# A transformer layer on eight cores: the attention output projection moved into the attention loop

## The reference

```python
x = x + attn(layernorm(x))        # x: (8, 2048, 2048), 16 heads of 128, 4 K/V heads
x = x + ffn(layernorm(x))
# attn: q, k = rotate(x @ w.T + b); v = x @ wv.T + bv
#   scores = q @ k.T * 128**-0.5 + tril(ones)    (added, so all 2048 keys count)
#   out = softmax(scores) @ v;  return out @ wo.T + bo
# ffn: gelu(x @ proj1.T + b1) @ proj2.T + b2     (hidden size 8192)
```

## Time and profile before

| | |
|---|---|
| median of 3 runs | 3598.46 us (3597.36 to 3599.26) |
| the profiled execution, its own time | 3603.3 us |
| its span, slowest of 8 cores | 3601.8 us (the others from 3589.8) |
| granted TensorE clock, mean by core | 0.964 to 0.967 |
| busy over the span | PE 3154.4 us (88%), DVE 1423.4 (40%), ACT 1010.7 (28%), POOL 37.6 (1%) |
| moved by DMA | 385.32 MB, 107 GB/s on average |

### The profile page before, as it was taken

How to read it: one execution, slowest core, us unless ns; L and a number is a source line. 1 busy time by engine, 2 the same in 40 slices (tenths; PEclk the granted TensorE clock), 3 DMA queues, 4 the chain that set the end, 5 groups by cost and what they waited for, 6 DMA issues and landing times.

```text
span 3601.8 us, 51951 instructions; the slowest of 8 cores (3589.8 to 3601.8 us)
## 1 busy us (share of the span) xinstructions
PE 3154.4 (88%) x19893; PEld 1623.8 (45%) x20240; DVE 1423.4 (40%) x2425; ACT 1010.7 (28%) x1836; POOL 37.6 (1%) x64
## 2 busy tenths in 40 slices
PE   4599978888888888994999999999819999999999
PEld 1244445556556555441444444444404444444444
DVE  2512247777777775224122231322241222312223
ACT  3334456666666663113100101001021001010010
POOL 1000000000000000000000000000000000000000
PEclk8799999999999999997999999999959999999999
DMA  5232200000000001761656656566726565565666
GB/s 198 85 82 76 76 24 2 2 2 2 2 2 2 2 2 50 203 171 47 158 155 149 151 150 152 151 152 168 210 88 156 150 152 150 152 152 152 151 162 190
DMA packets 622179, 385.32 MB, mean 107 GB/s; under 512 B 7153, under 2 KB 605553, under 8 KB 617842
## 3 DMA queue, kind: packets, MB, share of 16 engines
q1 hardware_dynamic: 613874, 348.42, 38.2%
q0 software_dynamic: 8064, 33.56, 2.6%
HBM read 356.79 MB, written 25.17 MB: 106 GB/s over the span
## 4 chain that ended last, share of the span: by engine, by line
PE 73%; ACT 10%; DVE 7%; issue 5%; DMA 3%; DVEq 0%; ACTq 0%; SPq 0%; POOLq 0%
PE psh L960 25%; PE pso L980 24%; PE psqk L411 8%; ACT xn L566 7%; PE pso L670 6%; PE pvps L529 6%; DVE xn L586 3%; PE ps_t L515 2%; DMA xstg<-xT 2%; PE psvt L362 1%; DMA xn<-r1T 1%; PE sc L505 1%; ACT qbuf L545 1%; DVE t L837 1%; DVE qbuf L840 1%
## 5 line engine op out<-in xcount | busy, mean ns | idle before, releaser
L960 PE MATMUL psh<-qbuf,p1bf 128*128 128x512 bf16 x4014 | 884.9, 380 | 80.9 <-DVE p1bf L903 76.4
L980 PE MATMUL pso<-qbuf,p2bf 128*128 128x512 bf16 x4014 | 880.8, 379 | 16.2 <-ACT qbuf L996 11.9
L960 PEld LDWEIGHTS psh<-qbuf,p1bf 128*128 128x128 bf16 x4096 | 401.6, 98 | 563.2 <-issue 82.8
L566 ACT ACTIVATE xn<-sc 128x896 bf16<-128x896 f32 (+7 forms) x736 | 553.5, 773 | 308.6 <-PE sc L505 255.4
L980 PEld LDWEIGHTS pso<-qbuf,p2bf 128*128 128x128 bf16 x4096 | 400.2, 98 | 496.8 <-issue 15.4
L996 ACT ACTIVATE qbuf<-psh,b1f 128x1024 bf16<-128x1024 f32 x128 | 142.6, 1114 | 1400.1 <-PE psh L960 1400.1
L903 DVE CAST p1bf<-p1stg 128x2048 bf16<-128x2048 f32 x128 | 156.9, 1227 | 691.6 <-PE psh L960 616.3
L937 DVE CAST p2bf<-p2stg 128x2048 bf16<-128x2048 f32 x128 | 157.1, 1227 | 620.6 <-PE pso L980 529.7
L505 PE MATMUL sc<-kbuf,qbuf 128*128 128x512 bf16 x897 | 265.5, 380 | 97.3 <-ACT xn L566 75.2
L586 DVE COPY xn<-ps_t 128x2048 bf16<-128x2048 bf16 x256 | 312.2, 1220 | 95.7 <-PE ps_t L515 95.7
L515 PE MATMUL ps_t<-ident_s,xn 128*128 128x128 bf16 x4096 | 270.8, 219 | 82.7 <-DVE xn L586 78.3
(11 more groups left out here) (86 smaller groups left out, 1146.4 us busy)
## 6 DMA issues: line engine op xcount, KB each, us to landing
p1stg<-p1T SPq DMA_DIRECT2D x128, 1024.0 KB, 8.5
p2stg<-p2T SPq DMA_DIRECT2D x128, 1024.0 KB, 6.3
wstg<-wqT SPq DMA_DIRECT2D x16, 1024.0 KB, 6.3
wstg<-woT SPq DMA_DIRECT2D x16, 1024.0 KB, 11.4
xblk<-xT SPq DMA_DIRECT2D x16, 1024.0 KB, 7.1
xstg<-xT SPq DMA_DIRECT2D x8, 1024.0 KB, 6.9
xstg<-xT POOLq DMA_DIRECT2D x8, 1024.0 KB, 6.6
wstg<-wvT SPq DMA_DIRECT2D x8, 1024.0 KB, 5.5
```

Source lines behind the costliest of these rows:

```text
L566: last = s.activation(p_sb[u % 3]()[:, il:ih], sc[sh][:, il - h0:ih - h0], AF.Exp, bias=f32(bias), scale=f32(D ** -0.5), accum_out=acc)
L960: ins = t.matmul(psh[hc % 2][:, sl], p1bf[hc % 2][:, c * 128:(c + 1) * 128], xn2[:, c * TH + ns * SWT: c * TH + (ns + 1) * SWT], start=(c ...
L980: ins = t.matmul(pso2[i % 2][:, sl], p2bf[i % 2][:, hc * 128:(hc + 1) * 128], hblk[:, hc * TH + ns * SWT: hc * TH + (ns + 1) * SWT], start ...
```

## The change

The output projection becomes 64 units: unit k makes output block k % 16 for the 512 tokens of slice k // 16, with 16 matmuls into one PSUM buffer `wops`. `u_of` gives the iteration of unit k: for the four slices the units start at u = 68, 132, 196 and 260 and follow at every third u. Iterations beyond 254 don't exist, so units 48 to 63 (`tail_units`) come after the loop. In the loop the cast of a unit's weights stands at u-2 on VectorE, the eviction at u+1 on ScalarE and the add of x at u+2 on VectorE. Each unit loads its own 1 MB of weights through SyncE, and 256 KB of x and stores 256 KB of the sum through GpSimd. To make room in PSUM the PV block has one buffer instead of two. The sum goes to DRAM whole, and each half of the feed-forward reads 8 MB of it back, 4 MB through SyncE and 4 MB through GpSimd. The old output projection stage is gone.

The V projection has two PSUM accumulators in place of eight: one pass over the token tiles, all weights loaded and cast once, by VectorE, before the first matmul, and all engines but SyncE wait at the barrier before it.

```diff
+    r1T = nc.dram_tensor("r1T", [C, T], F32, kind="Internal").ap()
     outT = nc.dram_tensor("outT", [C, T], F32, kind="ExternalOutput").ap()
...
-            full_barrier(skip_sync=True, skip=("tensor", "scalar"))
...
+            full_barrier(skip_sync=True)
...
+                    wvbf = esB0.enter_context(
+                        nc.sbuf_tensor("wvbf", [128, NCC * KVD], BF16))
                     psvt = [esB0.enter_context(
                         nc.psum_tensor(f"psvt{i}", [128, KVD], F32))
-                        for i in range(TPG)]
+                        for i in range(2)]
...
+                    def phB0_cast(v):
+                        for q in range(NQ):
+                            p.w(v, f"ld_w{q % 2}", 16 * (q // 2 + 1))
+                            p.inc(v.tensor_copy(
+                                wvbf[:, q * CPS * KVD:(q + 1) * CPS * KVD],
+                                wstg[q % 2][:, 0:CPS * KVD]), "s_pool")
+                    block.vector(phB0_cast)
+
+                    def phB0_pe(t):
+                        p.w(t, "s_dve", bB0["s_dve"])
+                        p.w(t, "s_pool", bB0["s_pool"] + NQ)
+                        for j in range(NT):
+                            p.w(t, "s_act", bB0["s_act"] + j - 1)
+                            for c in range(NCC):
+                                t.matmul(psvt[j % 2][:],
+                                         xn1[:, c * T + j * 128:c * T + (j + 1) * 128],
+                                         wvbf[:, c * KVD:(c + 1) * KVD],
+                                         start=(c == 0), stop=False)
+                            p.inc(t.matmul(psvt[j % 2][:], ones1[:], bvr_bf[:],
+                                           start=False, stop=True), "s_pe")
+                    block.tensor(phB0_pe)
+
+                    def phB0_act(s):
+                        for j in range(NT):
+                            p.w(s, "s_pe", bB0["s_pe"] + j + 1)
                             p.inc(s.activation(vTb[:, j * KVD:(j + 1) * KVD],
-                                               psvt[j % TPG][:], AF.Identity,
+                                               psvt[j % 2][:], AF.Identity,
                                                bias=f32(0.0)), "s_act")
-                        for hv in range(NPASS):
-                            for qq in range(NQP):
-                                cast(hv * NQP + qq)
-                                if qq == 1 and hv >= 1:
-                                    for j in range((hv - 1) * TPG, hv * TPG):
-                                        evac(j)
-                        for j in range((NPASS - 1) * TPG, NPASS * TPG):
-                            evac(j)
-                    block.scalar(phB0_sc)
-
-                    def phB0_pe(t):
-                        for g in range(NL):
-                            hv, qq = divmod(g, NQP)
-                            p.w(t, "s_pool", bB0["s_pool"] + g + 1)
-                            p.w(t, "s_dve",
-                                bA["s_dve"] + 5 + 2 * (CPS * qq + CPS - 1))
-                            if qq == 0 and hv > 0:
-                                p.w(t, "s_act", bB0["s_act"] + hv * TPG)
-                            for j in range(hv * TPG, (hv + 1) * TPG):
-                                for ci in range(CPS):
-                                    c = qq * CPS + ci
-                                    ins = t.matmul(
-                                        psvt[j % TPG][:],
-                                        xn1[:, c * T + j * 128:
-                                            c * T + (j + 1) * 128],
-                                        wbf[g % 2][:, ci * KVD:(ci + 1) * KVD],
-                                        start=(c == 0), stop=False)
-                            if qq == NQP - 1:
-                                for j in range(hv * TPG, (hv + 1) * TPG):
-                                    ins = t.matmul(psvt[j % TPG][:], ones1[:],
-                                                   bvr_bf[:], start=False,
-                                                   stop=True)
-                            p.inc(ins, "s_pe")
-                    block.tensor(phB0_pe)
+                    block.scalar(phB0_act)
...
-                pvps = [esC.enter_context(
-                    nc.psum_tensor(f"pvps{i}", [128, G * 128], F32))
-                    for i in range(2)]
+                pvps = esC.enter_context(
+                    nc.psum_tensor("pvps", [128, G * 128], F32))
+                wops = esC.enter_context(nc.psum_tensor("wops", [128, SW], F32))
+                xw = [esC.enter_context(nc.sbuf_tensor(f"xw{i}", [128, SW], F32))
+                      for i in range(2)]
+                tmpw = [esC.enter_context(
+                    nc.sbuf_tensor(f"tmpw{i}", [128, SW], F32)) for i in range(2)]
+                r1bw = [esC.enter_context(
+                    nc.sbuf_tensor(f"r1bw{i}", [128, SW], F32)) for i in range(2)]
                 bC = dict(p.cnt)
+                ldw_bC = [p.cnt["ld_w0"], p.cnt["ld_w1"]]
+                xsem = ["ld_xg", "ld_x1"]
+                bXG = [p.cnt["ld_xg"], p.cnt["ld_x1"]]
+
+                NTS = T // SW
+                NUNITS = NTS * NCC
+                af_need = lambda ts: (ts + 1) * (SW // 128) * KVH
+                u_of = lambda k: (4 * (af_need(k // NCC) - 1) + 8
+                                  + 3 * (k % NCC))
+                pe_at, act_at, cast_at, radd_at = {}, {}, {}, {}
+                tail_units = []
+                for k in range(NUNITS):
+                    uk = u_of(k)
+                    if uk <= NU - 2:
+                        pe_at[uk] = k
+                        act_at[uk + 1] = k
+                        cast_at[uk - 2] = k
+                        radd_at[uk + 2] = k
+                    else:
+                        tail_units.append(k)
...
+                def phC_sync(sync):
+                    for k in range(NUNITS):
+                        i = k % NCC
+                        p.w(sync, "s_pool", bC["s_pool"] + k - 1)
+                        p.inc(sync.dma_start(
+                            out=wstg[k % 2][:]
+                            .rearrange("p (c i) -> p c i", i=128),
+                            in_=woT[:, i * 128:(i + 1) * 128]
+                            .rearrange("(c p) i -> p c i", p=128)),
+                            f"ld_w{k % 2}", 16)
+                block.sync(phC_sync)
+
+                def phC_gp(g):
+                    def store(k):
+                        i, ts = k % NCC, k // NCC
+                        p.w(g, "s_dve", bC["s_dve"] + k + 1)
+                        p.inc(g.dma_start(
+                            out=r1T[i * 128:(i + 1) * 128,
+                                    ts * SW:(ts + 1) * SW],
+                            in_=r1bw[k % 2][:]), f"st_r1{k % 2}", 16)
+                    for k in range(NUNITS):
+                        i, ts = k % NCC, k // NCC
+                        p.w(g, "s_dve", bC["s_dve"] + max(k - 1, 0))
+                        p.inc(g.dma_start(
+                            out=xw[k % 2][:],
+                            in_=xT[i * 128:(i + 1) * 128,
+                                   ts * SW:(ts + 1) * SW]), xsem[k % 2], 16)
+                        if k >= 2:
+                            store(k - 2)
+                    store(NUNITS - 2)
+                    store(NUNITS - 1)
+                block.gpsimd(phC_gp)
+
+                def emit_unit(t, k):
+                    i, ts = k % NCC, k // NCC
+                    p.w(t, "s_pool", bC["s_pool"] + k + 1)
+                    p.w(t, "s_act_af", af_need(ts))
+                    p.w(t, "s_act", bC["s_act"] + k)
+                    for ca in range(NCC):
+                        ins = t.matmul(
+                            wops[:], wbf[k % 2][:, ca * 128:(ca + 1) * 128],
+                            attfm[:, ca * T + ts * SW:ca * T + (ts + 1) * SW],
+                            start=(ca == 0), stop=(ca == NCC - 1))
+                    p.inc(ins, "s_pe")
+
+                def emit_evac(s, k):
+                    i = k % NCC
+                    p.w(s, "s_pe", bC["s_pe"] + k + 1)
+                    p.w(s, "s_dve", bC["s_dve"] + max(k - 1, 0))
+                    p.inc(s.activation(tmpw[k % 2][:], wops[:], AF.Identity,
+                                       bias=bof[:, i:i + 1]), "s_act")
+
+                def emit_cast(v, k):
+                    p.w(v, f"ld_w{k % 2}", ldw_bC[k % 2] + 16 * (k // 2 + 1))
+                    p.w(v, "s_pe", bC["s_pe"] + max(k - 1, 0))
+                    p.inc(v.tensor_copy(wbf[k % 2][:], wstg[k % 2][:]),
+                          "s_pool")
+
+                def emit_radd(v, k):
+                    p.w(v, "s_act", bC["s_act"] + k + 1)
+                    p.w(v, xsem[k % 2], bXG[k % 2] + 16 * (k // 2 + 1))
+                    p.w(v, f"st_r1{k % 2}", 16 * (k // 2))
```

(116 more changed lines are left out.)

81 lines of the change are left out of this document (5 added, 76 removed).

## The result

The changed kernel is slower: 1.0189 times the time before, 95% interval 1.0177 to 1.0202, so 68 us on a median of 3598.9 us, or 3667 us; the times lie between 3661.5 and 3675.3. The forecast was 3648 us, 50 us slower, in a range of 3605 to 3690. The profiled execution took 3664.7 us against 3603.3 before.

A forecast was written before the change was run, and what follows sets the result against it. In attention, VectorE was taken to set the pace at 3.13 us a head, except where PV blocks delay transposes; elsewhere TensorE is nearly full. 23 + 142 - 108 - 7 = +50 us gave 3648 us, range 3605 to 3690.

The forecast's parts named there:

- V projection, +23: Before the first K matmul: V starting only after the barrier and weight casts costs 23 us (20 to 26).
- Attention, +142: Attention loop: 48 projection units at every third head cost 2.96 us each, 142 us in all.
- the in-order recurrence: Attention loop: copy times followed through TensorE's and VectorE's in-order queues; 12 heads take 54.2 us, today 42.4.
- double block: Attention loop: PV block and unit in the same place, once in 12 heads, 7.08 us on TensorE.
- Tail and read back, -108: Behind the loop to LayerNorm 2: 16 units at 6.5 us steps plus an 8 MB read back, 108 us saved (-125 to -85).
- Second half, -7: Second half's read back: split load lets its first 8 of 16 chunks go ahead, 7 us saved (-11 to +3).
- (a): Attention loop: takes the units nearly free, 3546 us at best; chance 0.11, partly or whole.
- (b): Attention loop: nothing hides, 5.3 us a unit, 3760 us; chance 0.05, shared with anything past the range's top.
- (c): Tail behind the loop: fast, TensorE bound at 4.3 us a unit, 26 us less, 3622 us; chance 0.10.
- (e): Attention loop: estimate a third too high, about 2 us a unit, 3602 us, no change; chance 0.04.
- (d): Tail behind the loop: every unit at the 1.2 GHz level, step 7.5 us, 3660 us; chance 0.15.

The follow-up runs named there:

- run 1: New V projection alone, put into the kernel before: 3616.8 us, against 3592 to 3596 us before in the same session.
- run 3: Changed kernel with units at every fourth head, halfway between PV blocks, 47 in the loop: ratio 1.001 to the kernel before.
- run 4: Changed kernel with each unit cut into three pieces at successive heads, cast and add at the PV head, 46 units in the loop: 3519.6 us.
- run 11: Changed kernel with 47 whole units, each directly behind a PV block: attention 1505.2 us, median span 3813.3 us.
- run 7: Changed kernel without the weight loads of 14 of the 16 units behind the loop: that stretch 103.7 us instead of 131.0, median span 3620.7 us.
- run 10: Changed kernel with units in pieces, old V projection and four instead of two weight staging buffers behind the loop: ratio 0.9757 to the kernel before.
- Run 8: Changed kernel with the sum read back in one 8 MB load on SyncE instead of two of 4 MB: 3664.7, 3668.5 and 3686.5 us.

## Why the prediction was right, point by point

- **V projection, +23: +21.6.** Shown by run 1. The cast chain ended 11.0 us after the normalisation (149.4 + 1.2 against 139.6 on core 7), where 12.0 was worked out; the start at the low clock cost 2.8.
- **Attention, +142: +151.5.** The step held: the in-order recurrence gave 54.2 us for 12 heads, and core 2 took 54.1 to 54.4 in four of its nine stretches of 12 heads, counted from the copy behind a double block. The others took 55.9 to 57.7. In them a step or two is 1.3 to 1.7 us longer: at 829.30 it is 9.20 in place of 7.58. There are seven such steps, 10.8 us together, and 142 and 10.8 make 152.8, where core 2 took 151.0 more than before. The term was mis-sized by what the forecast left out, the clock inside the loop. Core 2, timeline and then stretches:

```profile
828.44 4.75 PE L593 MATMUL pvps<-xn,vTb 128*128 128x128 bf16 x64
829.30 1.22 DVE L658 COPY xn<-ps_t 128x2048 bf16<-128x2048 bf16 x1
...
838.50 1.23 DVE L658 COPY xn<-ps_t 128x2048 bf16<-128x2048 bf16 x1 [5.99 <-PE ps_t L579]
```

```profile
820.00:824.00 4.00, 3.06 (x37) 2.13 (x36) 2.60 (x4) 3.93 (x12) 0.00 (x0) 1.00 0.04 5
824.00:828.00 4.00, 2.25 (x16) 1.36 (x17) 3.28 (x11) 3.29 (x9) 0.00 (x0) 0.89 0.73 196
828.00:832.00 4.00, 4.00 (x53) 4.00 (x51) 3.55 (x9) 0.07 (x1) 1.07 (x2) 0.68 0.42 99
832.00:836.00 4.00, 3.95 (x35) 2.39 (x34) 0.51 (x1) 0.00 (x0) 0.00 (x0) 1.00 0.33 102
```

  TensorE was busy for 2.25 of 4 us, and then ran at a granted clock of 0.68 in the block that everything waits for, which took 4.75 us in place of 3.74. The cores bear it out: attention took 1355.1 and 1355.6 us on the two cores whose clock fell five times, 1357.7 to 1359.3 on the five where it fell seven times, 1362.3 on the one with ten. That is some 1.4 us a fall, and with none it would be about 1348 us (an estimate, the line through these drawn on), where the forecast had 1207 + 142 = 1349. Runs 3, 4 and 11 show that the placement of the blocks, not the amount of work, made the cost: 48 units cost 3.2 us each at every third head, 47 cost 1.9 each midway between PV blocks, 6.3 behind them, and 0.1 in pieces.
- **Tail and read back, -108: -104.8.** The step behind the loop was forecast at 6.5 us; core 0 took (1664.74 - 1599.03) / 10 = 6.6, core 7 took 7.6, the median of the cores 7.0. Run 7 shows that the weights' transfers set it, run 10 that it is their bandwidth. That the sum came so close is in part luck: the last cast came 92 us after the last PV eviction's start where the forecast had 88, and the rest took 37 where it had 40. What was missing is the spread: the metric is the slowest core. This stage took 121 to 142 us over the cores where before it took 235.7 to 237.0, and the whole is 68 us slower where the medians give 60. But the stage alone does not explain these 8 us. In run 7 its cores lie within 7 us and yet end 21 us apart (3610.5 to 3631.6); attention, with its falls of the clock, takes 1352.0 to 1362.6 there, and differs by 7 us in the changed kernel, where it differed by 0.7 before. How the 8 us divide is open.
- **Second half, -7: -10.8.** Run 8 shows 7 us of it as the split's. The other 3 or 4 are left open. GpSimd's wait for its own store was taken too short: it issued 14.5 us after SyncE on core 7, where the forecast had about 8.
- **The range.** The ends that it names, 2.3 to 3.5 us a unit with steps of 5.0 to 7.5, add up to 3598 and 3686, not 3605 and 3690. The measured 3667 lies inside either way.
- **Rivals.** (a), the units nearly free, is false for whole units and true for pieces: TensorE's idle was enough, but in bits of under 2 us. (b) was false: 3.2 us, not 5.3. (c) was false, as the transfers hold the stage. (e), a third less in attention, was false: 3.2 us a unit, not 2. (d) holds in part: the granted clock was 0.87 over the stretch of core 0 shown in run 7, and of its 16 units four took 5.1 to 5.3 us and twelve 3.6. The Trainium skill's rule (TensorE: Matmul & The Clock Gate, on oscillation), that bursts behind a DMA wait start cold every time, agrees with the trace in part: on core 7 five of the six units that had waited more than 2 us for their weights took 5.3 to 5.8 us, the sixth, after 2.26 us, 3.61. But the casts there waited for transfers, not for TensorE, so the longer units cost nothing that these waits show; the clock cost in attention, where the forecast had not looked.

The changed kernel's time can so be given back: 22 to 25 us by the old V projection and 147 by the pieces, and what is left of the change, the projection inside the loop, is then worth 2.5%.

## What to carry to other kernels

Idle time of an in-order engine is worth something only in the lengths in which it comes: read the slack behind one block (here 2.05 us) from the timeline, and cut what is moved there to less than that. Put the second engine's added work where that engine waits (run 4 did both; neither was tried alone). Moving work from a stage with much reuse of its weights to one with little trades compute for transfers: 1 MB served 13.8 us of matmuls before and 3.45 after, and the part left outside the loop became bound by bandwidth.

## What was not expected of the hardware

The granted clock fell inside a loop in which TensorE never idled for more than 1.4 us at a time (core 2 of the changed kernel). It fell there seven times in some 140 heads, and each fall cost 1.3 to 1.7 us. With the units behind PV blocks, where the idle times reach 2.7 us, it fell in most periods (0.93 over the loop). With pieces and at every fourth head, and in the kernel before, it did not fall between the first and the last heads of the loop (1.00), though on core 2 the loop before has an idle time of 1.6 us: the longest single idle time does not tell the two apart. In each of the seven cases the fall came behind heads with little TensorE work: busy for 2.0 to 2.2 of the 4 us before it. Stretches as thin went by without a fall too, so what decides it is not shown.
